# Layer norm and router moved 16 tiles ahead of the attention, expert routing cut into pieces between the tiles of its second half, in a fused attention and mixture-of-experts block

## The reference, cut to what matters

```python
xn  = layernorm(x)                      # x: 4096 tokens x 256
q, k, v = xn @ Wq, xn @ Wk, xn @ Wv     # 16 heads of 16: 4 local, 12 linear
local   = softmax over a window of 128 keys and the 128 before it, causal
linear  = softmax(q) @ cumsum_64(k'v / sum k'),  k' = elu(k) + 1   # blocks of 64 tokens
attn    = concat(local, linear) @ Wo + bo
top_v, top_i = top_k(xn @ router_w.T, 2);  g = softmax(top_v)      # 8 experts
ffn     = sum over e of  g_e * (gelu(xn @ w1[e].T) @ w2[e].T)      # 256 -> 1024 -> 256
return x + attn + ffn
```

## Time and profile before

| what | value |
|---|---|
| median of 3 runs | 774.88 us (772.18 to 775.35) |
| the profiled execution, its own time | 772.42 us |
| its span, first to last instruction | 770.7 us |
| busy: PE / PEld / DVE / ACT / POOL | 657.8 / 526.0 / 476.3 / 413.7 / 400.2 us |
| mean granted TensorE clock | 0.948 of full speed |
| PE busy in 10 us at 310, 330, 350, 370 us | 0.90, 2.56, 1.09, 10.0 us |

### The profile page before, as it was taken

How to read it: one execution, slowest core, us unless ns; L and a number is a source line. 1 busy time by engine, 2 the same in 40 slices (tenths; PEclk the granted TensorE clock), 3 DMA queues, 4 the chain that set the end, 5 groups by cost and what they waited for, 6 DMA issues and landing times.

```text
span 770.7 us, 21990 instructions
## 1 busy us (share of the span) xinstructions
PE 657.8 (85%) x6626; PEld 526.0 (68%) x6627; DVE 476.3 (62%) x1589; ACT 413.7 (54%) x1197; POOL 400.2 (52%) x411
## 2 busy tenths in 40 slices
PE   0899999999899986221899999999999999999893
PEld 0566666666666654111788888888888888888672
DVE  3899998999999889883424444444444444434331
ACT  2677888888788875000534444554444554444441
POOL 2466676667767674462334554444554544444421
PEclk9999999999999998555989999999999999999997
DMA  5333333433343330001334444445445444534421
GB/s 150 97 111 111 124 109 113 145 122 110 109 141 125 116 102 23 15 12 31 64 53 80 81 74 79 70 71 79 79 76 79 73 70 77 81 61 57 64 31 22
DMA packets 85658, 63.36 MB, mean 82 GB/s; under 512 B 52371, under 2 KB 79252, under 8 KB 85620
## 3 DMA queue, kind: packets, MB, share of 16 engines
q1 hardware_dynamic: 71988, 43.96, 21.0%
q0 software_dynamic: 13632, 18.91, 16.8%
HBM read 36.08 MB, written 17.96 MB: 70 GB/s over the span
## 4 chain that ended last, share of the span: by engine, by line
PE 48%; issue 1%; SPq 1%; DVE 1%; DMA 1%; POOL 0%; ACT 0%; DVEq 0%; ACTq 0%; POOLq 0%
PE bank L399 25%; PE bank L1258 23%; SPq L1173 1%; DMA out<-attn,rows_to 0%; DMA stage<-stage 0%; POOL out L1201 0%; DVE stage L1344 0%; DVE attn L1373 0%; DVE wtokh L487 0%; DVE val L486 0%; DVE wtokh L490 0%; DVE wtokh L488 0%; DVE wtokh L485 0%; DVE val L489 0%; ACT stage L1285 0%
## 5 line engine op out<-in xcount | busy, mean ns | idle before, releaser
L399 PE MATMUL bank<-stage,w1h 128*128 128x256 f16 (+1 forms) x1248 | 199.5, 267 | 9.4 <-DVE stage L1344 5.2
L399 PE MATMUL bank<-stage,w1l 128*128 128x256 f16 (+1 forms) x624 | 164.6, 266 | 0.0
L1258 PE MATMUL bank<-w2h,pt 128*128 x568 | 154.9, 273 | 5.8 <-issue 4.6
L1258 PE MATMUL bank<-w2h,spare 128*128 x568 | 154.8, 273 | 0.0
L1258 PE MATMUL bank<-w2l,pt 128*128 x568 | 154.8, 273 | 0.0
L399 PEld LDWEIGHTS bank<-stage,w1h 128*128 x1248 | 115.2, 99 | 29.0 <-issue 11.9
L1304 ACT ACTIVATE pt<-ss 128x512 f16<-128x512 f32 (+1 forms) x78 | 41.8, 583 | 153.5 <-PE bank L1258 104.7
L1201 POOL DMA_INDIRECT out<-res,rows_to x36 | 57.5, 1598 | 101.0 <-DVE res L1373 43.5
L1201 POOL DMA_INDIRECT out<-attn,rows_to x35 | 55.9, 1596 | 90.5 <-DMA out<-attn,rows_to 40.4
L754 ACT ACTIVATE ss<-ss,negmax 128x256 f32<-128x256 f32 x128 | 63.5, 497 | 22.1 <-DVE negmax L966 22.1
L1297 ACT ACTIVATE spare<-bank 128x512 f32<-128x512 f32 (+1 forms) x78 | 43.6, 559 | 47.3 <-PE bank L399 42.1
(11 more groups left out here) (240 smaller groups left out, 1648.8 us busy)
## 6 DMA issues: line engine op xcount, KB each, us to landing
stage<-w1c SPq DMA_DIRECT2D x16, 512.0 KB, 3.7
stage<-w2c SPq DMA_DIRECT2D x16, 512.0 KB, 3.6
stage<-stage SPq DMA_TRANSPOSE x268
xin<-x SPq DMA_DIRECT2D x32, 128.0 KB, 2.1
xn_rows<-xn SPq DMA_DIRECT2D x32, 128.0 KB, 1.8
xb<-x SPq DMA_DIRECT2D x32, 128.0 KB, 3.2
out<-res SPq DMA_DIRECT2D x32, 128.0 KB, 3.5
out<-res,rows_to POOLq DMA_INDIRECT x36
```

Source lines behind the costliest of these rows:

```text
L399: ins = pe.matmul(dst, lhs(a, k), rhs(c, k), start=(n == 0), stop=(n == len(terms) - 1))
L1258: ins = pe.matmul(bY[h][:, 0:D], (hh, hl)[a][:, f, h * P:(h + 1) * P], (w2h, w2l)[c][:, DS(which * (FC * D) + f * D, D)], start=(f == a == ...
```

## The change

One program part instead of three, and all 35 steps written out. LEAD = 16.
- **Ahead.** Before step 0, x of tiles 0 to 15 is loaded in eight DMAs of two tiles, normalized, scaled by 256, split in halves (upper ACT, lower POOL), turned by PE (four f16 transposes) and copied to SBUF by ACT; then PE does the router of these 16 tiles. All this uses the space of expert weights that are not loaded yet. Step t then does this for tile t+16 (the turn for t+14, the router for t+13), until the tiles run out: steps 0 to 15, 2 to 17 and 3 to 18.
- **The rows** kept in DRAM for the experts are the two f16 halves in the 1024 bytes that were f32 xn, so ACT L1285, DVE L1355 and PE's turn of groups 0 and 1 go; all groups, 0 and 1 too, are turned by SP's DMA, which reads the gathered rows themselves. A gather therefore waits until the group two before is turned.
- **Routing** runs in pieces: scores and the first choice at the end of DVE's step 18, the second choice in 19, totals and gates in 20, ranks and block numbers in 21, slots in 22, one batch of one-hots in each of steps 23 to 30, rows and gathers in 31, experts in 32. The one-hots of a batch are 16 `tensor_scalar`s on DVE (8 of 128, 8 of 72 columns, f16) instead of two broadcast operations and one on POOL.

Cut to its core; `copy_turned` stands behind lrow, `upper_half` at the end of ACT's step, `router_of` and `route_table` behind PE's L828, the routing pieces behind the softmax of q; `turn_early`, the first two calls of `turn_rows` on SP, waits for the gather and for the last use of the space.

```diff
+LEAD = 16
+AHEAD, WEIGHTS_AT = LEAD // 2, 3
-        with nc.Block() as block:
+        with nc.Block() as block:
         def steps(eng, emit):
-            for t in range(HEAD):
-                emit(Step(eng, t // 2, t % 2))
-            with eng.Fori(HEAD // 4, (NT - 4) // 4) as n:
...
+            for t in range(NT + 3):
+                emit(Step(eng, t))
+        SCORED = NT + 2 - LEAD
+        (COPIED, SECOND, TOTALS, RANKS, SLOTS, HOT) = (SCORED, SCORED + 1, SCORED + 2, SCORED + 3, SCORED + 4, SCORED + 5)
+        TABLE = HOT + BATCHES
+        def route_onehots(dve, i):
+            dve.wait_ge(wide_in, 3)
+            for c in range(CH):
+                k, tile = (i * CH + c) // NT, (i * CH + c) % NT
+                dve.tensor_scalar(hot_pos[i % 2][:, c, :], sm["piota"], sm["pos"][:, k, tile:tile + 1], None, ALU.is_equal)
+                ins = dve.tensor_scalar(hot_blk[i % 2][:, c, :], sm["biota"], sm["blk"][:, k, tile:tile + 1],
+                                        sm["tok"][:, tile:tile + 1], ALU.is_equal, ALU.mult)
+            ins.then_inc(hot_in, 1)
             @block.sync
+                for q in range(3):
+                    load_ahead(q)
...
+                for q in range(3, AHEAD):
+                    load_ahead(q)
...
                 steps(sp, step)
+                groups(sp, turn_rows, first=2)
             @block.gpsimd
+                for q in range(AHEAD):
+                    rstd_of(2 * q, 2)
+                    if q:
+                        for t in (2 * q - 2, 2 * q - 1):
+                            lower_half(t)
+                    if q == 1:
+                        constants()
                 def step(t):
...
                     pool.tensor_tensor(xb[b][:], xb[b][:], bias[:], ALU.add).then_inc(s["xb_in"], 1)
+                    if t.early(LEAD - 1):
+                        lower_half(t.t + LEAD - 1)
...
                 def gather(i, m, ahead):
                     pool.wait_ge(e["from_in"], upto(i, m, ahead))
+                    pool.wait_ge(turned[n], 16 * 2 * KC * moved(i, m, ahead - 2))
             @block.scalar
                 def step(t):
 ...
+                    if t.early(LEAD - 2):
+                        copy_turned(t.t + LEAD - 2, b_xnt)
                     if t.has(0):
-                        act.activation(xth[b][:], b_xnt[:, 0:D], ACT.Copy, scale=XS).then_inc(s["xth_in"], 1)
...
 +                    if t.early(LEAD):
+                        upper_half(t.t + LEAD)
             @block.tensor
+                for t in range(LEAD):
+                    turn_x(t, bank[t % 2])
+                pe.wait_ge(pool_const, CONSTANTS)
+                pe.wait_ge(w_lo, len(jobs))
+                for t in range(LEAD):
+                    router_of(t)
                 def step(t):
 ...
+                    if t.early(LEAD - 3):
+                        router_of(t.t + LEAD - 3)
+                    if HOT < t.t <= HOT + BATCHES:
+                        route_table(pe, t.t - HOT - 1)
-                            ins = pe.transpose(b_xnt[:, k * P:(k + 1) * P], xn[b][:, k * P:(k + 1) * P], ident[:])
+                    if t.early(LEAD - 2):
+                        t.wait(s["rl_in"], LEAD - 2)
+                        turn_x(t.t + LEAD - 2, b_xnt)
             @block.vector
                 def step(t):
-                        dve.scalar_tensor_tensor(out=xtl[b][:], in0=b_xnt[:, 0:D], scalar=XS, in1=xth[b][:],
...
-                    if t.has(1):
-                        mean_of(t, 1)
-                    if t.has(1):
-                        variance_of(t, 1)
+                    if t.early(LEAD):
+                        mean_of(xin[u % 2][:, 0:D], u)
+                        variance_of(u)
+                        guarded(u, 1)
...
                         dve.reciprocal(rden[b][:, :, 1], cum0[b][:, 0:CTX:CTX - 1]).then_inc(s["rden_in"], 1)
-                    if t.has(1):
-                        normed(t, 1)
+                    if t.early(LEAD):
+                        scaled(xin[t.row(LEAD)][:, 0:D], t.t + LEAD)
+                    if HOT <= t.t < HOT + BATCHES:
+                        route_onehots(dve, t.t - HOT)
+                    if t.t == TABLE + 1:
+                        route_experts(dve)
                     if t.has(0):
                         t.wait(s["tok0"], 0)
...
 +                    if t.t == COPIED:
+                        route_first(dve)
+                    if t.t == SECOND:
+                        route_second(dve)
+                    if t.t == TOTALS:
+                        route_weights(dve)
+                    if t.t == RANKS:
+                        route_blocks(dve)
+                    if t.t == SLOTS:
                         route_slots(dve)
```

More of the change, by code:

```diff
@@ L613, in route_rows @@
[L613 to L621 removed]
+            ins = dve.tensor_tensor(sm["blk"], sm["rk"], sm["pos"], ALU.subtract).then_inc(slots_known, 1)
+            dve.wait_ge(slots_known, 1)
@@ new lines, in block_kernel @@
+        H = G // P
+        FQ = FC // 4
+        bH, bY = bank[1:5], bank[5:7]
+        xg = [[xin[0], xin[1]], [rows[0], rows[1]]]
+        yg = [[res[0], res[1]], [attn[0], attn[1]]]
+        xh = [view(stage[0], m * D, KC, G, dt=F16) for m in range(2)]
+        xl = [view(stage[0], (2 + m) * D, KC, G, dt=F16) for m in range(2)]
+        sel = view(qs[0], 0, H, E)
+        hid = [view(buf, q * FQ * G, FQ * G) for buf in (ss, small) for q in range(2)]
+        hh, hl = view(pt, 0, FC, G, dt=F16), view(spare[0], 0, FC, G, dt=F16)
@@ new lines, in columns, with moved, upto_half @@
+        def columns(i, m, ahead=0):
+            j = known(i, m, ahead)
+            return j + NPAIR if j is not None and j >= NPAIR else 4 * i + H * (m + ahead)
+        def moved(i, m, ahead=0):
+            j = known(i, m, ahead)
+            if j is None:
+                return H * (i + (m + ahead) // 2) + H
+            return sum(1 if g >= NPAIR else H for g in range(j % 2, j + 1, 2))
+        def upto_half(i, m, ahead, h):
+            j = known(i, m, ahead)
+            return upto(i, m, ahead) if not h or j is None else min(j, NPAIR - 1) + 3
@@ new lines, in groups, with upto, slot @@
+        def groups(run, emit, first=0):
+            for j in range(first):
+                emit(j // 2, j % 2)
+            with run.Fori(first // 2, (NPAIR - AFTER) // 2) as i:
+                for m in range(2):
+                    emit(i, m)
+            for j in range(NPAIR - AFTER, NG):
+                emit(j // 2, j % 2)
+        def upto(i, m, ahead=0):
+            return 2 * i + (m + ahead + 3)
+        def slot(i, m, ahead):
+            return (m + ahead) % 2, i + (m + ahead) // 2
@@ L952, in normed, with mean_of @@
[L952 to L962 removed]
+                def mean_of(src, t):
+                    dve.bn_stats(stats[t % 2][:], src).then_inc(s["stats_in"], 1)
@@ L1106, in halves @@
-        def halves(i, m, ahead=0):
-            j = known(i, m, ahead)
-            return 1 if j is not None and j >= NPAIR else H
-        def columns(i, m, ahead=0):
-            j = known(i, m, ahead)
-            return j + NPAIR if j is not None and j >= NPAIR else 4 * i + H * (m + ahead)
-        def moved(i, m, ahead=0):
-            j = known(i, m, ahead)
-            if j is None:
-                return H * (i + (m + ahead) // 2) + H
-            return sum(1 if g >= NPAIR else H for g in range(j % 2, j + 1, 2))
```

1144 lines of the change are left out of this document (566 added, 578 removed).

## The result

The changed kernel takes 860.95 us (median of 4 runs, 860.26 to 861.36) where the kernel before takes 774.15: ratio 1.1123, 95% interval 1.1097 to 1.115. The forecast was slower, 823 us, 780 to 842; the direction held, the time is 19 us above the range, 38 above the forecast.

A forecast was written before the change was run, and what follows sets the result against it. PE was taken to bound the experts, a DVE, ACT, PE loop of 8.6 us a step the attention. Terms -40.7 + 19 + 4.5 - 6.5 + 20 + 54 + 1 = +51 on 772.4 gave 823 us, range 780 to 842.

The forecast's parts named there:

- What bounds the kernel: Expert stage is PE work the change leaves alone, so what counts is what happens before it starts.
- The start: Before step 0: 16 tiles prepared first, with a 5 us rstd stall and 7 us of router matmuls; +19 us.
- Steps 0 to 15: First half of attention: new half-splitting work on ACT and POOL lengthens both loops to 8.85 to 8.9 us; +4.5 us.
- The two loops: Attention's chains of waits: DVE, ACT, PE, 8.6 us a step; and through POOL, 8.4 a step, 0.25 slack.
- Steps 16 to 31: Second half of attention: L957 (0.33 us) and the scores copy leave the DVE, ACT, PE loop; -6.5 us in 15 periods.
- The pieces: Routing pieces on DVE, steps 18 to 22: 15 us of uncovered work plus waits beside POOL; +20 us.
- The one-hots: Steps 23 to 30: batches in DVE's loop alternate with POOL's 4.9 us of work, 7 us a batch; +54 us.
- The rival on the clock: PE's granted clock falls to half in some ten long steps; +15 us, 838 us, chance 0.11.
- main case: All terms summed, with DVE's one-hots waiting for POOL at the SBUF port; 823 us, chance 0.50.
- The handover: From tile 31's L774 to the end of group 2's first layer: 59.5 us instead of 100.2; -40.7 us.
- The no-wait rival: f16 tensor_scalars on DVE pass beside POOL without waiting for the port; +9 to +14, 785 us, chance 0.22.
- The pace of the one-hots: DVE's own work for a batch of 16: 1.6 to 2.8 us, 2.1 taken; 1.5 by the skill's tier.

The follow-up runs named there:

- E13: E10 plus PE turning groups 0 and 1, the first 16 tiles' router matmuls in the first 16 steps, the one-hots' token product on POOL: 760.78 us, ratio 0.9789.
- E6: Changed kernel with xb loaded a step earlier, table matmuls at the end of PE's step and rrec ahead of pieces and one-hots: 797.34 us, ratio 1.0284.
- E1: Changed kernel with SyncE's load of xb issued one step earlier, ahead of the wait for POOL's stage_lo: 848.09 us, ratio 1.0955.
- E3: Changed kernel with DVE's reciprocal rrec ahead of the routing pieces and one-hots instead of behind them: 853.74 us, ratio 1.1024.
- E10: E7 plus DVE's copy of the first probabilities on ACT from step 18 and ACT's exponential of the gates one step later: 781.21 us, ratio 1.0055.
- E4: Changed kernel without POOL's two stage operations from step 23 on, a memset of the low halves in their place: 841.01 us, ratio 1.085.
- E2: Changed kernel with PE's table matmuls at the end of its step and the sums of the tables one step later: 833.26 us, ratio 1.0772.
- E5: Changed kernel with 100 unread matmuls of 62 columns on PE ahead of each wait for the one-hots: 853.03 us, ratio 1.1012.
- E7: E6 plus, from step 18 on, POOL's two stage operations ahead of its atl, cum and xb: 788.06 us, ratio 1.0164.

## Why the prediction was wrong, point by point

- **What bounds the kernel**: right. The expert stage took 377.4 us again, and everything was decided before it.
- **The start, +19**: +17.5, in part by luck. The 96 router matmuls took 2.6 us (34.09 to 36.69 in the changed kernel) where 7 had been taken, and DVE's waits for POOL's rstd ahead of step 0 were 2.1 us where 5 had been; so the rest cost more than forecast. It wasn't tested part by part; moving the matmuls away gave 1.3 us (E13).
- **Steps 0 to 15, +4.5 (0 to +10)**: +14.4. The two loops cost less than forecast: without the third the stage is at +1.5 to +1.9 (E6, E1), in steps of 8.68 us. The step that failed is "both loops come to 8.85 to 8.9": L743 was put into POOL's loop, but that loop was read as waiting for ACT only. With 0.67 us more the one through SyncE's queue, the end of L838, three issues, a landing of 3.6 us, closes at 9.3. It had no slack in the kernel before (POOL L697 waited for xb, 0.32 us at 189.51), and moving L743 ahead of L836 was the place to ask what is queued behind stage_lo. The late landing in step 11, some 5 us, was not to be foreseen from the rows.
- **Steps 16 to 31, -6.5**: not found. The two steps without routing took 17.2 us in E1 and E6, as before. The step that failed is "PE ... get lighter but aren't in it": in E6 DVE was busy for 13.1 of these 17.2 us instead of 16.0, but PE for 16.5 instead of 15.6, with a single wait of 0.8 us, so PE's own work set them. The term was also too large for the prediction's own second loop, which it gave 0.25 us of slack a step against the 0.43 taken. Whether the later steps gained it can't be seen, since none stands without routing; this stays open.
- **The pieces, +20 (+11 to +27)**: +27.7, where +17.8 was forecast with the lighter loop. Their own work was sized well. The working ("ahead of L982", 0.5 us covered) saw that PE needs rrec, but priced only the delay of DVE. PE's step stands meanwhile and DVE then waits for the odd scores (E3, 8.8 us), and ACT's wait for the second choice, not in the working at all, holds lrow (E10, 3.6 us in its step).
- **The one-hots, +54 (+13 to +62)**: +66.1, where +50.5 was forecast. Two errors of opposite sign, so that this term is nearer than its working. The first is the place: "They stand between L1019 and L1025, in the loop" is false, they stand behind the softmax of q (L1402 of the changed kernel). The prediction let the batch start beside L691 and pay all of POOL's 4.9 us, 7 us a batch. In fact it starts with POOL in L838 and meets only that and ke, and takes 3.4 to 5.3 us; E4 measures that wait, 2.1 us a step. "The two alternate", read from the earlier trace rows, holds where both have work (E13). The second is PE: its part of the loop was left at 1.7 us, and its wait for the table was not followed to what is queued behind it; from the last one-hot to DVE's masked scores it is 4.9 to 5.7 us in the changed kernel. That was 27.8 us (E2) alone, and 41.8 together with rrec (E6 against the changed kernel).
- **The rival on the clock** had been kept apart with 0.11. It isn't a rival but a part of the main case: E5 shows 2.3 us and more of it in a step. Added to the 823 us of the main case it would have given 838.
- **The handover, -40.7**: -37.8, by the steps written. The last result was stored 22.4 us behind step 31's line (442.38) instead of 19.6, which is all of the difference. From there it went as forecast: PE waited for group 0's turns to 454.5 and group 1's first layer started at 464.8.
- **The no-wait rival** was summed too high: its own terms (13 to 22 us for the one-hots, 14 for the pieces) give +4 to +13, not +9 to +14. E4's steps and the held operations rule it out in any case.
- **The pace of the one-hots**: 2.96 us a batch against the 2.1 taken and the upper bound of 2.8. In E13 both one-arithmetic forms have a pitch of 0.155 us, with 128 columns and with 72; with a second arithmetic step and a second pointer the 72-column one had 0.21. Columns hardly count at this size. The Trainium skill's tier (VectorE: DVE Perf Modes, the perf-mode tier table), by which the batch was an estimated 1.5 us, doesn't carry over to operations this small. The same page of the Trainium skill (The TRN2 errata) has a fixed extra cost for each instruction with an SBUF source. That 128 and 72 columns have the same pitch agrees with a fixed cost; its size here is larger than that page's table gives, an estimated 0.09 us against 0.155.

The 38 us by which the time exceeds the forecast are thus 10 of the first half, 10 of the pieces, 16 of the one-hots and 2 of the rest. In all three stages one kind of wait was missed: not the one that a new operation has, but that of the work queued behind the engine that waits for it. In the one-hots a wrong place for the batch hid part of it.

## What to carry to other kernels

When work is slipped into the steps of a pipeline, follow for each new wait the queue of the engine that waits, down to the next thing that another engine needs; put the consumer at the end of its step, and what others wait for (a small reciprocal, a load) ahead of the new work. A DMA behind a wait on an engine's queue is part of that engine's loop with its landing time: 0.67 us more on POOL cost 9 to 12 us in 16 steps until the load was issued a step earlier. Read the place of a new operation in the kernel itself, and ask which operations of the other engine are still ahead of it there: that decides what it can collide with. And when a wait is moved, look where it went: E7 took 1.9 us out of the batch and 0.75 out of the step. Several such waits lie one behind the other, so remove them together before judging the design: single gains of 13, 28 and 7 us made 64 together, and six more moves turned a version that was 11% slower into one that is 2% faster than the original.

## What the runs showed of the hardware

- **DVE against POOL in SBUF goes by whole operations, by turns.** A `tensor_scalar`, or a `tensor_tensor` with two SBUF inputs, is held to the end of the POOL operation beside it: L499 2.13 us instead of 0.24 at 301.83, L457 of 8 columns 2.11 at 254.90, three one-hots in a row beside three POOL operations in E13. With POOL idle they run freely, so a batch loses only to those POOL operations that are still to come. A reciprocal isn't held (E6, L1391, 0.17 us at 298.96, beside L838 from 298.91). A DVE `tensor_reduce` from SBUF isn't held either: L411 took 0.41 us at 216.21, beside POOL's L838 (216.17 to 218.29), and L412, with two SBUF inputs, 1.92 behind it. The Trainium skill (SBUF — State Buffer, Who interferes with whom) says just this: the shared port pair is a lock held for the whole instruction, and `tensor_reduce` never contends on trn2.
- **The granted clock** is at 2.4 GHz for one 14 us step (1.00) and partly at 1.2 GHz in the next (0.72 over 18 us), with the same program in both (E5's stretches). PE's work between the last one-hot and the masked scores took 3.34 us at the one level and 5.66 at the other.
